# Moving where x is loaded, and the order of the side work, in a fused state-space and coupling layer

## The reference, cut to what matters

```python
# 16 batches of x[1024 tokens, 256 features]; all arithmetic in float32
def attn(x):                                   # a selective state-space layer
    xi, res = split(x @ W_in.T + b_in)         # 512 channels each
    xi = silu(causal_conv4(xi) + b_conv)       # 4 taps, by channel
    delta, B, C = split(xi @ W_x.T + b_x)      # 512, 16, 16; delta through softplus
    h = exp(delta * A) * h + delta * B * xi    # along the tokens, 512 x 16 states
    y = (h * C).sum(states) + xi * D
    return (y * silu(res)) @ W_out.T + b_out
def ffn(x):                                    # a coupling network, 3 cycles
    gf = global_net(x.mean(tokens))
    for _ in range(3):                         # 4 small matmuls with gelu, then sigmoid
        x = x + (0.1 + range * (0.7 * gf + 0.3 * coupling_net(x) - 0.5) * 2) * twist(x)
    return x
x = layernorm(x + attn(x)); x = layernorm(x + ffn(x))
```

## Time and profile before

| | us |
|---|---|
| median of 3 runs | 4040.12 (4036.9 to 4040.94) |
| the profiled execution, its own time | 4040.28 |
| its span, first to last instruction | 4038.5 |
| start of unit 0 on GpSimd | 60.40 |
| unit 256 to unit 320 on GpSimd, one period | 1010.85 to 1249.29 |
| start of the last unit on GpSimd | 3896.56 |
| TensorE's granted clock over the span | 0.946 |

### The profile page before, as it was taken

One profiled execution on the slowest core, in us unless ns is written; L12 is line 12 of the kernel. 1 busy time (PEld: TensorE's weight loads), 2 busy tenths in 40 slices (PEclk: granted clock), 3 DMA queues, 4 the chain that ended last, 5 costly groups with the idle time before them and its releaser, 6 DMA issues. The chain is left out here.

```text
span 4038.5 us, 51729 instructions
## 1 busy us (share of the span) xinstructions
PE 3524.4 (87%) x18776; PEld 1611.5 (40%) x18776; DVE 3429.6 (85%) x2508; ACT 2959.0 (73%) x3918; POOL 3644.6 (90%) x1604
## 2 busy tenths in 40 slices
PE   7669989899998998989898998989989898897766
PEld 3224353443434344353443434344353443434233
DVE  4988988889898898989889898898989889898861
ACT  4447868778786877868777786877868777785753
POOL 4999999999999999999999999999999999999860
PEclk9779999999999999999999999999999999998888
DMA  5354373543536354373644546454363544546320
GB/s 182 130 175 154 128 230 120 188 152 130 186 130 224 129 191 138 122 229 120 197 148 155 159 152 200 140 187 129 133 218 123 194 149 158 160 138 199 127 86 31
DMA packets 329645, 630.04 MB, mean 156 GB/s; under 512 B 27952, under 2 KB 226608, under 8 KB 329136
## 3 DMA queue, kind: packets, MB, share of 16 engines
q1 hardware_dynamic: 329392, 626.74, 47.0%
HBM read 456.76 MB, written 169.87 MB: 155 GB/s over the span
## 5 line engine op out<-in xcount | busy, mean ns | idle before, releaser
L1060 POOL TENSOR_TENSOR work<-u_q,b_quad 128x1024 f32<-128x1024 f32 x1024 | 2397.3, 2372 | 138.2 <-DMA u_q<-u_scratch 97.1
L816 ACT ACTIVATE da<-delta_q,neg_a 128x1024 f32<-128x1024 f32 x1024 | 1126.3, 1112 | 600.9 <-DVE work L995 430.8
L987 DVE TENSOR_TENSOR_SCAN da<-da,work 128x1024 f32<-128x1024 f32 x608 | 1389.9, 2286 | 151.4 <-ACT da L816 119.7
L1067 POOL TENSOR_TENSOR work<-work,c_quad 128x1024 f32<-128x1024 f32 x416 | 985.2, 2368 | 11.6 <-DVE work L987 11.3
L987 DVE TENSOR_TENSOR_SCAN work<-da,work 128x1024 f32<-128x1024 f32 x416 | 945.9, 2278 | 29.9 <-ACT da L816 28.1
L727 PE MATMUL y_sum<-work,v_all 128*32 128x256 f32 x8192 | 613.3, 399 | 303.3 <-POOL work L1067 190.7
L995 DVE TENSOR_TENSOR work<-da,c_quad 128x1024 f32<-128x1024 f32 x608 | 743.9, 1224 | 28.6 <-DMA c_quad<-bc_scratch 4.6
L752 ACT ACT_TABLE_LOAD x563 | 722.3, 1283 | 14.5 <-DMA v_all<-in_vectors 3.9
L727 PEld LDWEIGHTS y_sum<-work,v_all 128*32 128x32 f32 x8192 | 199.8, 110 | 771.0 <-issue 259.3
L613 PE MATMUL banks<-xi,w_all 128*128 128x512 f32 x1024 | 479.8, 612 | 9.4 <-ACT g_act L797 5.1
L600 PE MATMUL banks<-xi,taps 128*128 128x512 f32 x984 | 453.2, 606 | 0.0
(11 more groups left out here) (86 smaller groups left out, 3270.3 us busy)
## 6 DMA issues: line engine op xcount, KB each, us to landing
delta_q<-delta_scratch SPq DMA_DIRECT2D x256, 512.0 KB, 5.8
u_q<-u_scratch SPq DMA_DIRECT2D x256, 512.0 KB, 6.1
delta_scratch<-delta SPq DMA_DIRECT2D x64, 512.0 KB, 2.9
u_scratch<-soft SPq DMA_DIRECT2D x64, 512.0 KB, 2.9
b_quad<-bc_scratch SPq DMA_DIRECT2D x64, 512.0 KB, 4.7
c_quad<-bc_scratch SPq DMA_DIRECT2D x64, 512.0 KB, 7.1
s_quad<-res_scratch SPq DMA_DIRECT2D x128, 256.0 KB, 4.1
y_scratch<-s_quad SPq DMA_DIRECT2D x128, 256.0 KB, 3.2
```

What stands on the lines that cost most here:

```text
L816: act.activation(da[:, t % 2, :], delta_q[:, slot, :], ACT.Exp, scale=neg_a[:, t % PERIOD:t % PERIOD + 1]).then_inc(da_ready, 1)
L987: dve.tensor_tensor_scan(dst, da[:, t % 2, :], work[:, slot, :], 0.0, ALU.mult, ALU.add) \
L1060: pool.tensor_tensor(work[:, slot, :], u_q[:, copied, :], b_quad[:, j, :], ALU.mult) \
L1067: pool.tensor_tensor(work[:, un % WORK, :], work[:, un % WORK, :], c_quad[:, un % PHASE, :], ALU.mult) \
```

## The change

Six things are changed.

1. x for the residual is loaded into `big` instead of `oT`, as soon as the e tasks of the batch before have read `big`; ScalarE's first write to `oT` now waits for the output stores instead.
2. In the o task the matmuls with x and b_out come first, and the wait for `yg` behind them; in the e task the matmuls with `residual` and `oT` come ahead of the wait for the last multiplication.
3. GpSimd's update is cut into halves of 512 tokens: four instructions instead of two, each pair behind the multiplication of its half, and the next cycle's matmuls wait for their half.
4. The first convolution is 3.5 blocks of 4 on VectorE, the half that is left on TensorE.
5. GpSimd does 25 products in a period instead of 26, at other positions.
6. Many tables have other numbers.

```diff
-POOL_AT = (1, 4, 6, 8, 9, 10, 11, 12, 16, 18, 21, 24, 28, 32, 33, 36, 42, 44, 49, 52, 55, 56, 58, 59, 60, 61)
+POOL_AT = (0, 4, 5, 8, 9, 11, 16, 17, 22, 25, 26, 28, 32, 33, 41, 42, 46, 49, 52, 55, 56, 58, 59, 60, 61)
...
-E_AT = (57, 58, 59, 61)
+E_AT = (57, 58, 60, 61)
...
-RES_IN_AT = 28
-XRES_AT = 66
-OUT_AT = (64, 64)
-XFEAT_AT = 48
+RES_IN_AT = 48
+XRES_AT = 62
+OUT_AT = (61, 63)
+XFEAT_AT = 49
...
-BY_VECTOR, BY_TENSOR = ((0, SEQ), (1, SEQ), (2, L)), 3
+BY_VECTOR, BY_TENSOR = ((0, SEQ), (1, SEQ), (2, SEQ), (3, L)), 1
...
-        x_res = oT[:, :, :].rearrange("p m t -> p (m t)").rearrange("p (k c) -> p k c", c=DM)
+        x_res = x1
...
                     if f == 0:
-                        sp.wait_ge(first_stored[DC - 1], 64)
+                        sp.wait_ge(first_stored[1], 64)
+                        sp.wait_ge(first_stored[2], 64)
                     if f:
-                        for h in range(2):
-                            sp.wait_ge(out_done[h], 32 * f)
+                        sp.wait_ge(e_ready, 4 * f)
...
                 if kind == "o":
-                    pe.wait_ge(yg_in[n % 2], 64 * (2 * f + n // 2 + 1))
                     if n == 0:
                         pe.wait_ge(xr_in, 16 * (f + 1))
                     for r in range(2):
                         tb = 2 * n + r
                         half = shared[:, r * DM:(r + 1) * DM]
+                        pe.matmul(half, eye, x_res[:, tb, :], start=True, stop=False)
+                        pe.matmul(half, eye, b_out, start=False, stop=False)
+                        if r == 0:
+                            pe.wait_ge(yg_in[n % 2], 64 * (2 * f + n // 2 + 1))
                         for k in range(4):
-                            pe.matmul(half, yg[:, n % 2, k, r * P:r * P + P], w_out[:, k, :], start=k == 0, stop=False)
-                        pe.matmul(half, eye, b_out, start=False, stop=False)
-                        mm = pe.matmul(half, eye, x_res[:, tb, :], start=False, stop=True)
+                            mm = pe.matmul(half, yg[:, n % 2, k, r * P:r * P + P], w_out[:, k, :],
+                                           start=False, stop=k == 3)
...
                         if c:
-                            pe.wait_ge(updated, (CYCLES - 1) * f + c)
+                            pe.wait_ge(updated, 2 * ((CYCLES - 1) * f + c - 1) + half + 1)
...
                             cycle = CYCLES * f + c
-                            pool.wait_ge(f_prod, 2 * cycle + 2)
-                            pool.tensor_tensor(oT[:, 0, :], oT[:, 0, :], big[:, 1, :], ALU.add)
-                            pool.tensor_tensor(oT[:, 1, :], oT[:, 1, :], big[:, 0, :], ALU.subtract).then_inc(updated, 1)
+                            for half in range(2):
+                                cols = slice(half * L, half * L + L)
+                                pool.wait_ge(f_prod, 2 * cycle + half + 1)
+                                pool.tensor_tensor(oT[:, 0, cols], oT[:, 0, cols], big[:, 1, cols], ALU.add)
+                                pool.tensor_tensor(oT[:, 1, cols], oT[:, 1, cols], big[:, 0, cols], ALU.subtract) \
+                                    .then_inc(updated, 1)
```

49 lines of the change are left out of this document (27 added, 22 removed).

## The result

The changed kernel took 4047.14 us (median of 20 runs, 4028.29 to 4058.24), the kernel before on the same chip 4037.36 (4032.63 to 4044.76). The ratio is 1.0022, 95% interval 1.0014 to 1.0031: slower by 0.2%, where I had forecast 2.2% faster.

A forecast was written before the change was run, and what follows sets the result against it. GpSimd and VectorE were taken as two chains holding each other. 14 periods x 4.9 = 68.6, first and last period 2.3 each, head 1.1, tail 14.3: 88.6 off 4040.3 gives 3951.7, range 3915 to 4025.

The forecast's parts named there:

- SP's order at position 16: Moved SP issues: u_q of units 4 and 20 later, GpSimd waits 0.7 and 1.5, VectorE 0.5, between 0 and 4.
- rival of the queue: Batch boundary: c_quad takes 14 instead of 7.1, u_q of unit 20 lands 4 late; +4.3 a period, 4080; chance 0.08.
- The gate of position 8: VectorE's 3.42 us wait for the fold shrinks by 2.3 a period, between 0 and 3.4; new c_quad wait 1.3.
- The statistics: VectorE's waits a period: 2.7 less for o tasks, 2.0 less for statistics of the third e task.
- The sum by the later engine: One period summed by VectorE (236.2) and by GpSimd (235.2); the later decides, 236.2 instead of 241.1.
- GpSimd's price of a half update: Update instructions of 512 tokens on GpSimd take 1.24 each, adding 0.6 a period.
- Position 56: GpSimd's 2.63 us wait there goes wholly, as u_q is issued ahead of the feature load.
- Head: Start of the kernel: TensorE's softplus product begins at 33.8 instead of 37.52; 1.1 gained, between 0 and 3.7.
- Tail: After the last period: earlier x, early matmuls and half updates gain 14.3, between 9 and 19.
- Only the count counts: Rival: VectorE's removed waits come back at the next place; a period gains only 1.7, 3996; chance 0.24.
- Exclusive operations: Rival: VectorE products cannot run beside GpSimd instructions; 16 moved ones wait 2.3 each, 37 in all, 3989; chance 0.02.
- Half instructions cost a whole: Rival: GpSimd's half updates add 8.6 a period, 243.8, +2.7; 4063; chance 0.04.

The follow-up runs named there:

- ust11: Changed kernel with the store of the first u of a batch at position 11 instead of 9; 0.9905 of the kernel before.
- res_yg: Changed kernel with the fourth yg load at position 8 instead of 10 and the first block's res_scratch stores at 4 instead of 9; 0.9893 of the kernel before.
- side_back: Changed kernel with the coupling's first tasks and the x, v and r tasks at the positions of the kernel before; 0.9975 of the kernel before.
- old_tables: Changed kernel with every position table of the kernel before, 26 products among them; 0.9963 of the kernel before.
- old_pool25: old_tables with the 25 GpSimd product positions of the changed kernel; 0.9963 of the kernel before.
- pool_back: Changed kernel with the 26 GpSimd product positions of the kernel before; 1.0172 of the kernel before.
- uq4_early: Changed kernel with the second u_q load of a block at 13 instead of 15; 0.9925 of the kernel before.
- best: Changed kernel with the numbers of res_yg, uq4_early and side_back put back, and the x1 stores at 15 and 16 instead of 10 and 11; 0.9854 of the kernel before.
- sp_back: Changed kernel with SP's positions for yg, delta_q and u_q loads and x1, delta, u and first res_scratch stores as before; 1.0016 of the kernel before.
- bound_back: Changed kernel with the old batch boundary, except the e tasks, the norm of o and the bc_scratch store; 1.0201 of the kernel before.
- yg_only: Changed kernel with the fourth yg load at position 8 instead of 10; 0.9923 of the kernel before.

## Why the prediction was wrong, point by point

**SP's order at position 16: the step that failed.** For the moved issues I counted 0.7 at unit 4 and 1.5 at unit 20, "behind the load of x and behind a store that waits for the norm of o", and looked at SP's order only around the boundary and position 48. The stretch from the store of `u` to the load of `u_q` was not read. It measured 5.5 at unit 16 and 2.0 at unit 4; `ust11` and `res_yg` show that putting this order right gives 1.2 to 1.3%. At the two units that I named GpSimd waits 2.6 (2.0 and 0.6), close to my 2.2 and within its bound of 0 to 4; unit 16 was in no term, and with it the sum is 8.1. That the fourth `yg` load behind the same store makes the last o task late was in no term either. My rival of the queue had the mechanism, a DMA issued behind others, but named the boundary and unit 20; its 4080 was 33 us above the result.

**The coupling's place: a term put at nothing.** The new positions of the x, r, t and coupling tasks were in neither sum. VectorE's wait for ScalarE's exp rose from 2.1 to 4.4 us a period at unit 20 and from nothing to 2.7 at unit 24; `side_back` gives 0.5%.

**The gate of position 8.** The wait went (54.5 for all gates, from 110.6), and nothing was gained: VectorE arrives late by what it waits for `c_quad`. In the changed kernel those waits are 3.8 a period (61.6 in all), not 1.3, the first of them at the product of position 1, which I had not considered:

```profile
1009.60 1.23 DVE L1002 TENSOR_TENSOR work<-da,c_quad 128x1024 f32<-128x1024 f32 x1 [2.05 <-DMA c_quad<-bc_scratch]
1018.33 1.23 DVE L1002 TENSOR_TENSOR work<-da,c_quad 128x1024 f32<-128x1024 f32 x1 [1.77 <-DMA c_quad<-bc_scratch]
```

Two terms of my sum, -2.3 and +1.3, were one chain: the fold is ready at a fixed time, and who comes later waits less. `old_tables` shows besides that the x load in `big` does not touch this gate.

**The statistics.** Those of the third e task wait no more, as forecast. Those of the o tasks were forecast to lose 2.7; at position 13 they lost 1.3, at 15 they gained 1.0 and wait 2.4, since the fourth `yg` load comes 6.6 us later (55.1 against 48.5 in a period). By themselves the new o order was no gain in a period.

**The sum by the later engine.** I added up removed waits on each engine and took the larger remainder. Neither sum held: GpSimd had 3.5 more of idle time a period instead of 4.2 less, and VectorE's waits, which I had falling by 6, rose from 26.0 to 26.9. I had named idle time of VectorE that stays at 26 as a sign of being wrong, with 3996 as the time; it stayed, and the time was 4047. A removed wait on one engine did not shorten the other's wait for `u_q`, and came back on its own engine at the exp of units 20 and 24 and at `c_quad`. (VectorE is 3.3 late at scan 62 and 0.3 at scan 63, but only because the statistics that stood between the two now come behind the second.)

**GpSimd's price of a half update.** 1281 and 1284 ns against 1.24 forecast; the busy time is as in the sum. Position 56: the wait of 2.7 is gone, right. Unit 0: 2.1 became 0.5, right but for 0.5. `b_quad`: not gone, 1.4 at unit 2. At position 28 I had left the wait as it was; the product of unit 25 stands there now.

**Head.** The softplus product starts at 34.12 (forecast 33.8) and takes 8.80 (forecast 9.67). But unit 0 starts at 60.5, 0.1 later: the stores of `bc_scratch`, for which the `b_quad` loads wait, now stand behind the first `u_q`, which waits for the store of `u`, and `b_quad` is issued at 55.58 instead of 53.86. `u` was stored 1.7 earlier (48.30 against 50.01), and these 1.7 us were lost in SP's order again. The first period gained 9.7 instead of 2.3. Its start, before and after: on VectorE the product of unit 0 waits for `c_quad`, with scan 1 behind it; on GpSimd it holds no scan back.

```profile
70.52 1.23 DVE L995 TENSOR_TENSOR work<-da,c_quad 128x1024 f32<-128x1024 f32 x1 [4.61 <-DMA c_quad<-bc_scratch]
71.66 2.28 DVE L987 TENSOR_TENSOR_SCAN work<-da,work 128x1024 f32<-128x1024 f32 x1
```
```profile
62.96 2.29 DVE L994 TENSOR_TENSOR_SCAN work<-da,work 128x1024 f32<-128x1024 f32 x1 [17.11 <-ACT da L820]
65.26 2.30 DVE L994 TENSOR_TENSOR_SCAN da<-da,work 128x1024 f32<-128x1024 f32 x1
```

By unit 2 that lead is down to 1.9; the rest comes later in the period, and `old_pool25` against `old_tables` shows 8.8 from the product table. From the other side, `pool_back` against the changed kernel, the table is worth only 4.3 there (222.7 against 218.4).

**Tail.** Forecast 14.3, measured 13.1. TensorE's wait for the first update, 7.00 in the earlier trace rows, is 3.85, twice; the updates follow each other 3.3 sooner (forecast 3.5):

```profile
3935.17 3.78 PE L637 MATMUL banks<-w_all,yg 128*128 128x256 f32 x8 [5.57 <-DMA yg<-y_scratch]
...
3984.43 8.79 PE L685 MATMUL banks<-oT,w_all 128*128 128x512 f32 x16 [3.85 <-POOL oT L1085]
```

I had named "no wait of TensorE for x" as a sign; it waits 3.81 for x all the same, and then comes the first row, the term that fell short: TensorE waits for `yg`, which SP issues behind output stores that wait for the last norm. From the last fold (3905.44 before, 3923.74 after) to the end of the o tasks it is 38.4 before and 33.8 after, 4.6 instead of 6.3. The e task's early matmuls gave 0.9 (forecast 1.0), from the last product of the coupling to the end 20.2 and 19.3.

**The rivals.** "Only the count counts", the second likeliest, had VectorE's idle time right, which stayed, and its 3996 was 51 us off: no period gained 1.7, here or in `old_pool25` (0, with other positions as well). "Exclusive operations" finds no support: the two engines are busy 214.78 and 225.66 of 244.37 us side by side. "Half instructions cost a whole" is refuted by 1281 ns.

**Left open.** How a lead at scan 16 grows on its way to the end of the period (1.3 becomes 1.8 in `uq4_early`, 1.7 becomes 2.5 in `ust11`); why the 26 old products are 1.5% worse in the new order, beyond that GpSimd then waits for softplus; what a product less is worth by itself; and where the last 1.8 us between `best` and the forecast period are.

## What to carry to other kernels

Where one queue issues both the store and the reload of a value just made, read everything between the two: nine small issues there cost 1.2% of this kernel against the same nine moved ahead of the store, into time spent waiting for the value. A removed wait is a gain only if the engine did not arrive late anyway: add waits along the chain of one engine, position by position, not by kind, and at each meeting of two chains ask which is done later. Tables that were made together are put back together or by single numbers: half-way mixtures (`sp_back`, `bound_back`, `pool_back`) measured their own collisions.

## What the runs showed that I had not expected

A table with one product less on GpSimd, 2.0 us of an engine 90% busy, was worth 0 in a full period and 8.8 us in the first (`old_pool25`). Three single-number edits (`ust11`, `yg_only`, `uq4_early`) each give 1.0 to 1.2%, and `res_yg` and `uq4_early` together no more than `res_yg` alone. A store of 512 KB and its reload by the same queue took 2.9 us from issue to issue in the kernel before (1063.32 to 1066.26) and 4.0 in `ust11`, and a GpSimd update of 128x512 takes 1.28 us against 2.35 for 128x1024, 0.54 of it.
